# Row maximum, subtraction and exponential of the attention scores taken tile by tile in a vision transformer block

## What is computed

```
h = tokens(x)                                     # 12608 x 192
q, k, v = split(layernorm(h) @ w_qkv)             # 12 heads of 16
scores = q . k[n-6 .. n+6] * 16**-0.5             # 13 keys per query, within the image
p = softmax(scores)                               # maximum, subtraction, exp, sum
h = h + (p . v) @ w_proj + b_proj
top 2 of 8 experts by layernorm(h) @ router_w.T, weights renormalised
h = h + sum_e w_e * (gelu(layernorm(h) @ w1[e] + b1[e]) @ w2[e] + b2[e])
```

## Time and profile before

| what | value |
|---|---|
| median of 3 runs | 1504.67 us (1501.07 to 1510.52) |
| the profiled execution | 1504.9 us, span 1503.1 us |
| PE busy | 1396.8 us, 93% of the span |
| DVE busy | 1121.1 us, 75% |
| POOL busy | 912.9 us, 61% |
| ACT busy | 664.4 us, 44% |
| granted TensorE clock, mean | 0.987 of full speed |

### The profile page before, as it was taken

One profiled execution on the slowest core, in us unless ns is written; L12 is line 12 of the kernel. 1 busy time (PEld: TensorE's weight loads), 2 busy tenths in 40 slices (PEclk: granted clock), 3 DMA queues, 4 the chain that ended last, 5 costly groups with the idle time before them and its releaser, 6 DMA issues. The chain is left out here.

```text
span 1503.1 us, 50698 instructions
## 1 busy us (share of the span) xinstructions
PE 1396.8 (93%) x17454; PEld 1162.3 (77%) x17455; DVE 1121.1 (75%) x2824; ACT 664.4 (44%) x1148; POOL 912.9 (61%) x900
## 2 busy tenths in 40 slices
PE   5999999998999999999788999999999999999995
PEld 4788888887888888888666677777777777777774
DVE  2579888898898888899677867666666666666663
ACT  2455455455555455455554433333333333333331
POOL 4236666666666666666367865666666556655565
PEclk9999999999999999999899999999999999999998
DMA  5565665766675675765355575555555545555543
GB/s 176 177 190 160 169 205 151 204 163 188 168 209 159 179 195 155 196 167 163 74 103 97 108 131 77 77 77 73 74 75 75 74 73 73 74 74 74 72 70 32
DMA packets 305660, 189.14 MB, mean 126 GB/s; under 512 B 201977, under 2 KB 291397, under 8 KB 304477
## 3 DMA queue, kind: packets, MB, share of 16 engines
q1 hardware_dynamic: 241706, 118.06, 32.1%
q0 software_dynamic: 41680, 41.84, 18.7%
q10 hardware_dynamic: 22115, 27.08, 5.7%
HBM read 89.79 MB, written 65.29 MB: 103 GB/s over the span
## 5 line engine op out<-in xcount | busy, mean ns | idle before, releaser
L502 POOL DMA_INDIRECT sorted_scratch<-payload,place x212 | 223.2, 1053 | 56.7 <-issue 56.3
L1143 PE MATMUL near<-we,both_patches 128*120 128x192 f32 x1272 | 224.5, 334 | 17.3 <-DMA both_patches<-in_xt 17.3
L1143 PEld LDWEIGHTS near<-we,both_patches 128*120 128x120 f32 x1272 | 208.7, 186 | 28.0 <-issue 27.2
L487 POOL DMA_INDIRECT out<-both_patches,token x111 | 199.8, 1800 | 36.5 <-issue 36.1
L487 POOL DMA_INDIRECT out<-v_side,token x108 | 197.4, 1827 | 37.6 <-issue 36.5
L577 ACT ACTIVATE stage<-near,bias 128x384 f32<-128x384 f32 x103 | 60.0, 582 | 359.6 <-PE near L1095 331.0
L1110 PE MATMUL qk<-w_hi,stage 128*128 x666 | 163.9, 246 | 4.4 <-DVE v_side L915 4.4
L1110 PE MATMUL qk<-w_hi,both_patches 128*128 x648 | 160.0, 247 | 5.0 <-issue 4.4
L1112 PE MATMUL qk<-w_hi,we 128*128 x666 | 163.8, 246 | 0.0
L1111 PE MATMUL qk<-w_lo,stage 128*128 x666 | 163.8, 246 | 0.0
L1112 PE MATMUL qk<-w_hi,both_patches 128*128 x648 | 159.6, 246 | 0.0
(11 more groups left out here) (264 smaller groups left out, 3611.7 us busy)
## 6 DMA issues: line engine op xcount, KB each, us to landing
both_patches<-in_xt SPq DMA_DIRECT2D x53, 720.0 KB, 5.0
v_diag<-v_scratch SPq DMA_DIRECT2D x159, 89.2 KB
v_scratch<-v_side SPq DMA_DIRECT2D x53, 191.2 KB, 3.8
tabs<-tab_scratch SPq DMA_DIRECT2D x53, 180.0 KB, 4.8
out<-h ACTq DMA_DIRECT2D x52, 180.0 KB
stage<-in_w ACTq DMA_DIRECT2D x8, 1152.0 KB
k_diag<-qk SPq DMA_DIRECT2D x436, 15.8 KB
stage<-in_w ACTq DMA_DIRECT2D x8, 576.0 KB
```

The costliest lines, as they stand in the source:

```text
L487: pool.indirect_dma_start(out=out, out_offset=bass.IndirectOffsetOnAxis(ap=token[k][:, n:n + 1], axis=0), in_=y[k % 2][:, n, :], in_offset ...
L502: pool.indirect_dma_start(out=sorted_dram, out_offset=bass.IndirectOffsetOnAxis(ap=at, axis=0), in_=payload[0:rows, 2 * (block % RING) + n ...
L1143: ins = pe.matmul(near[0:ROWS, n * D:n * D + D], patches[f % 2][:, x, n * ROWS:n * ROWS + ROWS], we[:, x, :], start=(x == 0), stop=(x == K ...
```

## The change

In DVE's step the two loops are merged: maximum of tile 0, subtraction of tile 0, maximum of tile 1, subtraction of tile 1. The wait for the transposes of the block before goes by tiles as well. ACT's exponential is split into two of 504 columns, each of which waits for its own subtraction and counts `exp_set` up. PE waits for the first half of the exponential before the four transposes of tile 0, and for the second before those of tile 1. Nothing else changes; the numbers computed are the same.

```diff
                 def exponentials():
 
-                    act.wait_ge(s["shifted"], 2 * (c + 1))
-                    act.activation(flat, flat, ACT.Exp, scale=DH ** -0.5 / (WS * WS)).then_inc(s["exp_set"], 1)
+                    for n in range(2):
+                        half = flat[:, n * HEADS * KEYS:(n + 1) * HEADS * KEYS]
+                        act.wait_ge(s["shifted"], 2 * c + n + 1)
+                        act.activation(half, half, ACT.Exp, scale=DH ** -0.5 / (WS * WS)).then_inc(s["exp_set"], 1)
...
                         dve.wait_ge(s["scored"], 2 * a + n + 1)
                         dve.tensor_reduce(mx[:, n], scores[:, n, 0:HEADS * KEYS].rearrange("p (h c) -> p h c", c=KEYS), AX.X, ALU.max)\
                            .then_inc(s["max_set"], 1)
-                    need(dve, s["prob_turned"], 2 * a)
-                    for n in range(2):
+                        need(dve, s["prob_turned"], 2 * a - 1 + n)
                         dve.wait_ge(s["max_set"], 2 * a + n + 1)
                         dve.tensor_tensor(prob[:, n], scores[:, n, 0:HEADS * KEYS].rearrange("p (h c) -> p h c", c=KEYS),
                                           mx[:, n].unsqueeze(2).to_broadcast([128, HEADS, KEYS]), ALU.subtract).then_inc(s["shifted"], 1)
...
-                    pe.wait_ge(s["exp_set"], c + 1)
                     for n in range(2):
+                        pe.wait_ge(s["exp_set"], 2 * c + n + 1)
                         for m in range(QUADS):
                             ins = pe.transpose(scores[0:VKEYS, n, 128 * m:128 * m + 128],
```

## The result

The changed kernel takes 1510.68 us (median of 12 runs, 1505.14 to 1517.78) against 1504.68 us for the kernel before (12 runs): ratio 1.0043, 95% interval 1.0023 to 1.0063. It is 6 us slower; the interval allows 3.5 to 9.5 us.

The account below looks back on a forecast made before the run. The pace was taken to be set by a loop through the exponential's end. Odd steps 2.5, even steps 2.9 and the last four 0.4 us gave +5.8 on 1504.9: 1510.7 us, 8-in-10 range 1500 to 1519.

Parts of the forecast that it names:

- PE's first wait: PE waiting for the exponential before its transposes: tile 0 comes after 0.68 us instead of 1.10, so 0.42 us earlier.
- What is late next: PE's wait for the router's payload from POOL (L514) grows as PE arrives 0.42 us earlier; gain counted as zero.
- The DMA issues hold the exponential: ACT's four own DMA issues (L603), not the subtraction, release the exponential, so its first half starts no earlier.
- The split of the exponential: On ACT, two halves last 1.13 us against 1.04: 0.09 us later at the end of every exponential, bounds 0 and 0.20.
- so again 0.09 counts: In 11 even steps POOL's L514 holds a small DVE instruction until L514 ends, so each step lengthens by 0.09 us.
- DVE's new order: DVE's two maxima and two subtractions last 0.23 us longer, 2.67 us instead of 2.44, paid only in steps without cover.
- +0.11 us at two joints: On DVE, each subtraction directly behind its maximum loses the 0.08 us overlap and adds a 0.03 us gap.
- The loop that sets the pace: From exponential through cast, POOL's payload, PE, logits and DVE back to ACT's DMA issues; contains the exponential's end, not its middle.
- The list of steps: Steps sorted by what covers DVE's delay, eleven even ones held by POOL, each charged 0.09 or 0.23 us: +5.8 us.
- My sign of being wrong: Steps changing length by more than 0.3 us would mean POOL and DVE meet in another order than assumed.
- The Trainium skill's rule: A semaphore between two VectorE instructions costs nothing extra; DVE's reordering would then cost 0, giving 1509.3 us in all.
- both costs arrive in full: Rival: the exponential's 0.09 and DVE's 0.23 us add up in all 49 steps, +15.7 us, 1520.6 us; chance 12%.

Follow-up runs that it names:

- e3: The changed kernel, but PE waits for both halves of the exponential before its first transpose: 1.0060 of the kernel before, 1512.21 us.
- e11: The kernel before with only the exponential in halves, PE waiting for both halves before its first transpose: 1.0005 of the kernel before, 1502.99 us.
- e8: The changed kernel with PE's transposes of the router's payload moved behind the first 5 of 15 q and k products: 1.0011 of the kernel before, 1506.60 us.
- e5: The kernel before with all twelve key transfers of a step issued by SP, none by ACT: 1.0141 of the kernel before, 1526.50 us.
- e6: The changed kernel with all twelve key transfers of a step issued by SP, none by ACT: 1.0135 of the kernel before, 1524.33 us.
- e1: The kernel before with DVE's new order alone, the exponential and PE's wait as before: 1.0064 of the kernel before, 1513.42 us.
- e2: The kernel before with the exponential in halves and PE's wait by tiles, DVE's order as before: 1.0015 of the kernel before, 1505.75 us.
- e10: A repeat run: the kernel before with the exponential in halves and PE's wait by tiles, DVE's order as before: 0.9996 of the kernel before, 1502.25 us.
- e9: The changed kernel measured again on another chip: 1.0052 of the kernel before, 1508.45 us.

## Why the prediction was right, and which of its terms were not

The time (1510.7 predicted, 1510.68 measured) and the direction are right, and so is the mechanism of the missing gain. That the time agrees to hundredths is luck: the interval is 6 us wide, and two terms were off in opposite directions.

- *PE's first wait.* Right: 0.68 us instead of 1.10, and the wait roughly halved (22.1 to 10.4 us).
- *What is late next.* Right: the payload's wait took it back in the same steps (8.0 to 21.4 us), the spacing became 2.56 to 2.59 us, and e3 and e11 found nothing measurable for the early start. e8 added what I hadn't said: behind the payload stands a second copy that hangs on the exponential just as much, so there was no single wait to be moved.
- *The DMA issues hold the exponential.* Right for the changed kernel and by e5 and e6. What I missed is how near the subtraction stood; in e1 it takes over in 23 of 45 steps. I also took the 2.44 us of the earlier trace rows for the rule: the four issues last up to 3.86 us before the change.
- *The split of the exponential.* Right in size (1.14 us for the two, 1.13 worked out), wrong in what reaches the end. This was 4.4 of my 5.8 us, "+0.09 us at the end of every exponential" in 49 steps; e2, e10 and e11 measure +0.15, -0.04 and +0.05%, so about 1 us and at most some 5. The step that failed is "so again 0.09 counts" for the eleven even steps in which POOL holds DVE: there a later L514 lets one more small DVE instruction through, and the held step gets 0.16 us shorter (medians of e2 and e10 against before). Only the odd steps pay, some 0.06 us each. I had looked at this alignment only for DVE moving later against POOL, not for POOL moving later against DVE.
- *DVE's new order.* Mis-sized. "+0.11 us at two joints" measured 0.19 each (2.83 to 2.84 us instead of 2.67 for the four, in 43 of 45 steps), but behind `xn` 0.18 us of the 0.39 is left, less than the 0.23 I counted. What was too small is the number of steps: I charged it in four odd and four even ones and, in part, in t = 22. In the changed kernel's profile the 16 even steps without a hold last 14.16 us instead of 13.99, and the held ones 0.23 us more than with the halves alone. Its share of the total was 1.4 us; by e9 and e10 it is 6 us, that is, practically the whole of the change's cost.
- *The loop that sets the pace.* "It contains the exponential's END" holds for the odd steps and, through POOL, for the held ones. In most even steps without a hold DVE alone sets the pace.
- *The list of steps.* The sum took eleven held steps from one profile. Which steps are held changes from one execution to the next: 8 in e2 and 9 in e10, which are the same kernel, and 7 and 8 in the two profiles of the changed one. My sign of being wrong, steps that change their length by more than 0.3 us, did come up, in 20 of the 45 steps. It decides nothing: e2 and e10 differ by that much in 15.
- *The Trainium skill's rule* ("VectorE: DVE Perf Modes", section "The DRAIN you can't avoid"), that a semaphore between two VectorE instructions costs nothing extra, isn't what e1 shows: 0.39 us more for the same four instructions, and 9.6 us at the end. Both orders have the same waits; in the old one another instruction stands between a maximum and its subtraction, and the wait is free.

So two errors offset each other: the split counted too high by about as much as DVE's order was counted too low. The rival "both costs arrive in full" (1520.6) was wrong in the sum, but right for DVE's order when it stands alone. What stays open is how L502 lengthens the first instruction of `xn`, and whether the early start is worth nothing or a few us.

## What to carry to other kernels

Before a wait on the busiest engine is counted as a gain, list everything behind it that hangs on the same late instruction. Here the half of the probabilities came 0.42 us earlier, but the cast and the copies that PE needs next stand behind the whole exponential on ACT, and the halves bought nothing. Putting a producer directly ahead of its consumer on one engine cost 0.19 us a joint here; one independent instruction in between (the other tile's maximum or subtraction) had hidden it. And a term that is real in most steps (0.09 us in 33 of 45) need not reach the end; only taking the parts of a change singly showed which of them was paid for.

## What the runs showed of the hardware that I had not expected

A VectorE instruction that waits for the maximum just ahead of it starts 0.10 to 0.11 us behind its end (342.35 to 342.46 in e1), where the one behind the reciprocal L1023 needed 0.03; independent ones overlap by 0.08. An instruction that stands behind a DMA issue of its own engine and waits for a semaphore as well can be put down in the profile to the semaphore's engine although the issue ended last: 52.7 us of the changed kernel's idle time ahead of L609 stand under DVE L1041, whose first half was ready over a microsecond before in the step shown:

```profile
L609 ACT ACTIVATE prob<-prob 128x504 f32<-128x504 f32 x88 | 50.0, 615 | 119.5 <-issue 66.8 <-DVE prob L1041 52.7
```

And whether a small VectorE instruction started 0.05 us ahead of POOL's L514 or 0.03 us behind its start went with 0.19 or 0.92 us for it, which makes a delay of under 0.1 us on one engine a gain on another. Beside POOL's L502 the first instruction of `xn` took 0.59 us instead of 0.37 when it started 0.53 us ahead of L502's end, but not when it started 0.15 us ahead of it.
